# Turning B and X of a selective-scan mixer by VectorE and DRAM, and another order of work for three cross-attention tiles

## The reference, cut to what matters

```
xp = pad(x @ W_in[:1536].T)                       # C, B, X: 512 features each
conv_out = sum(xp[:, k:k+s, :] * conv_w[:, k] for k in range(4)) + conv_b
C_, B_, xin = split(conv_out)                     # 16 heads of 32
Y = ssd(xin, A, B_, C_)[0] / norm                 # scan of batch entry 0, rated for each of 2
x = ln(x + Y @ W_out.T)                           # x1
x = ln(x + softmax(q(x) k(ctx).T) v(ctx) @ o_w)   # x2
x = ln(x + slots_and_experts(x))
```

## Time and profile before

| | us |
|---|---|
| median of 3 runs | 1476.79 (1472.14 to 1482.0) |
| profiled execution, its own time | 1479.82 |
| its span, first to last instruction | 1478.0 |
| PE busy in the span | 1314.2 (89%) |
| DVE / ACT / POOL busy | 731.9 / 442.8 / 218.3 |
| mean granted TensorE clock | 0.935 |

### The profile page before, as it was taken

One profiled execution on the slowest core, in us unless ns is written; L12 is line 12 of the kernel. 1 busy time (PEld: TensorE's weight loads), 2 busy tenths in 40 slices (PEclk: granted clock), 3 DMA queues, 4 the chain that ended last, 5 costly groups with the idle time before them and its releaser, 6 DMA issues.

```text
span 1478.0 us, 25849 instructions
## 1 busy us (share of the span) xinstructions
PE 1314.2 (89%) x10117; PEld 773.0 (52%) x10117; DVE 731.9 (50%) x1450; ACT 442.8 (30%) x1159; POOL 218.3 (15%) x182
## 2 busy tenths in 40 slices
PE   7999999999998899999999989877667766779998
PEld 4777777777675676767777554211111111126553
DVE  1655666666786778788888742000000000004665
ACT  2335443444323434434444330000000000002544
POOL 1122210222021222122222210000000000002221
PEclk9999999999999999999999999887877778789999
DMA  9452443432567698788887678999999999994773
GB/s 344 162 158 54 118 116 87 127 105 83 156 178 226 208 296 232 230 245 235 252 243 238 185 272 349 416 416 427 426 424 427 426 428 424 426 418 143 220 230 119
DMA packets 133353, 379.50 MB, mean 257 GB/s; under 512 B 15675, under 2 KB 52667, under 8 KB 116104
## 3 DMA queue, kind: packets, MB, share of 16 engines
q1 hardware_dynamic: 128456, 363.51, 69.9%
q10 hardware_dynamic: 4800, 14.68, 3.1%
HBM read 310.77 MB, written 67.37 MB: 256 GB/s over the span
## 4 chain that ended last, share of the span: by engine, by line
PE 58%; DMA 25%; DVE 7%; issue 2%; ACT 2%; SPq 1%; POOL 1%; ACTq 0%; DVEq 0%; POOLq 0%
DMA all_ring<-in_e_Wg 21%; PE mxw_bank L184 10%; PE mix_scores L730 7%; PE mxw_bank L982 5%; PE mix_scores L1759 4%; PE mxw_bank L1019 4%; PE mxw_bank L2243 4%; PE mxw_bank L1048 4%; PE mxw_bank L1067 2%; PE mix_scores L1782 2%; PE mix_scores L2276 2%; PE mxw_bank L2276 2%; PE mxw_bank L1009 1%; DMA all_space<-scratch_probs 1%; PE mxw_bank L722 1%
## 5 line engine op out<-in xcount | busy, mean ns | idle before, releaser
L1759 PE MATMUL mix_scores<-all_ring,all_space 128*32 128x512 f32 x968 | 150.4, 722 | 76.3 <-DMA all_ring<-in_e_W 38.1
L1809 DVE TENSOR_TENSOR all_space<-all_space 128x512 f32<-128x512 f32 x16 | 11.1, 694 | 380.6 <-ACT all_space L1818 380.6
L184 PE MATMUL mxw_bank<-all_ring,all_space 128*128 128x256 f32 x768 | 179.8, 388 | 1.7 <-DMA all_space<-in_WinT 1.7
L184 PEld LDWEIGHTS mxw_bank<-all_ring,all_space 128*128 128x128 f32 x768 | 145.3, 193 | 33.3 <-issue 10.8
L1818 ACT ACTIVATE all_space<-mix_scores 128x512 f32<-128x512 f32 x32 | 19.1, 597 | 409.4 <-PE mix_scores L1768 409.4
L1759 PEld LDWEIGHTS mix_scores<-all_ring,all_space 128*32 128x32 f32 x968 | 31.2, 120 | 179.4 <-DMA all_ring<-in_e_Wg 68.1
L254 DVE SCALAR_TENSOR_TENSOR all_ring<-all_ring,all_space 128x256 f32<-128x256 f32 x192 | 84.5, 482 | 76.6 <-ACT all_ring L203 74.3
L1782 PE MATMUL mix_scores<-all_ring,all_space 128*32 128x512 f32 x480 | 112.7, 735 | 10.2 <-DVE all_space L1812 10.2
L1242 POOL TENSOR_TENSOR all_space<-all_space,all_more 128x1232 f32<-128x1232 f32 x32 | 72.6, 2268 | 326.9 <-DVE all_more L1157 326.9
L1019 PE MATMUL mxw_bank<-all_space 128*128 128x512 f32 x248 | 113.1, 599 | 2.1 <-ACT all_space L1135 2.1
L730 PE MATMUL mix_scores<-all_space,all_ring 128*128 128x512 f32 x240 | 105.4, 592 | 0.0
(11 more groups left out here) (313 smaller groups left out, 2061.2 us busy)
## 6 DMA issues: line engine op xcount, KB each, us to landing
all_ring<-in_e_W SPq DMA_DIRECT2D x55, 2048.0 KB, 24.7
all_ring<-in_e_Wg SPq DMA_DIRECT2D x28, 2048.0 KB, 26.2
scratch_probs<-all_more SPq DMA_DIRECT2D x32, 768.0 KB, 3.5
all_space<-scratch_probs SPq DMA_DIRECT2D x64, 256.0 KB
all_ring<-in_xT SPq DMA_DIRECT2D x8, 1024.0 KB, 9.2
all_ring<-scratch_rates SPq DMA_DIRECT2D x64, 128.0 KB, 4.3
all_z<-in_x SPq DMA_DIRECT2D x16, 512.0 KB, 5.2
scratch_x1T<-all_more SPq DMA_DIRECT2D x128, 64.0 KB, 1.8
```

Of the source, the lines that this page charges most:

```text
L184: last = nc.tensor.matmul(bank[:, i * BT:(i + 1) * BT], hold["win"][:, k, m * P:(m + 1) * P], hold["xT"][b % 2][:, k, :], start=(k == 0), ...
L1759: last = nc.tensor.matmul(bank[w][q * ROWS:(q + 1) * ROWS, :], hm[u][:, k, :], weights[k % 2][:, q * FQ:(q + 1) * FQ], start=(k == 0), sto ...
```

## The change

**Mixer.** For blocks 1 to 7 (chunks 2 to 15), PE no longer turns B and X. DVE turns all eight tiles of a block in 32 x 32 pieces with one instruction (`turn_block`, 128 x 2048), SP stores the result to a scratch tensor in four DMAs, waits for them, and loads two arrays of 128 x 1024, one for each chunk (`exchange`). ACT's `take_b` and DVE's `weigh_x` then read SBUF instead of PSUM. Chunks 0 and 1 stay with PE. So that B is there early, the pairs of a block come in the order X, B, C. DVE adds the taps of each pair one place later in the order of work, and ACT normalises behind its second pair; the exceptions for the last two chunks are gone. **Cross.** Steps 2 and 3 have an order of their own on PE and DVE, with scores one tile further ahead; ACT's queries move; the statistics of the last two chunks move; SP loads the probabilities of tile 2 ahead of storing turned x2 of tile 0. **Semaphores.** Some are merged; this changes no order.

```diff
-PAIRS = ((8, 9), (10, 11), (0, 1), (2, 3), (4, 5), (6, 7))
+PAIRS = ((8, 9), (10, 11), (4, 5), (6, 7), (0, 1), (2, 3))
...
+    def exchange(sp, b):
+        sp.wait_ge(s["tok_turned"], b)
+        to = io["tok"][b * BT:(b + 1) * BT, :].rearrange("(j f) n -> f j n", f=QUAD)
+        for a in range(HG):
+            sp.dma_start(to[:, :, a * BT:(a + 1) * BT], turned[a * HD:(a + 1) * HD, :, :, :].rearrange("f j m n -> f j (m n)")).then_inc(s["tok_stored"], 16)
+        sp.wait_ge(s["tok_stored"], 16 * HG * b)
+        for c in (2 * b, 2 * b + 1):
+            wait_later(sp, s["xs_done"], c - 1)
+            wait_later(sp, s["btok_done"], c - 1)
+            sp.dma_start(tok[c % 2][:].rearrange("p a m f -> p (a m f)"), io["tok"][c * P:(c + 1) * P, :]).then_inc(tok_in[c % 2], 16)
...
+    def turn_block(dve, b):
+        dve.wait_ge(s["convX"], NX * (b + 1))
+        dve.wait_ge(s["convCB"], NCB * b + 2)
+        wait_later(dve, s["tok_stored"], 16 * HG * (b - 1))
+        nc.vector.transpose(turned[:], hold["conv"][b % 2][:, GROUPS:, :].rearrange("p m (j t) -> p j m t", t=QUAD)).then_inc(s["tok_turned"], 1)
...
                 first["weigh_x"](dve, c)
                 first["mask_scores"](dve, c)
-                taps(q)
+                taps(q - 1)
+                if c % 2:
+                    first["turn_block"](dve, c // 2 + 1)
                 first["rate_outputs"](dve, c)
                 first["advance_state"](dve, c)
-                if c == END - 2:
-                    taps(q + 1)
+                taps(q)
                 if c:
                     first["norm"](dve, c - 1)
-                if c != END - 2:
-                    taps(q + 1)
+                taps(q + 1)
                 first["residual"](dve, c)
                 if c >= 2:
                     first["turn_rows"](dve, c - 2)
-                taps(q + 2)
...
+                if known(t, 3):
+                    turn_probs(dve, t + 1)
+                    add_tokens(dve, t - 3, 1 - u, 0)
+                    turn_x2(dve, t - 1, 1 - u)
+                    take_scores(dve, t + 2, False)
+                    first["norm"](dve, LATE_ROWS[t])
+                    slot_maxima(dve, t - 2, 0)
+                    denominators(dve, t + 2)
+                    residual(dve, t, u)
+                    slot_sums(dve, t - 2, u, 0)
+                    return
...
                 if t in LATE_ROWS:
                     first["normalise"](act, LATE_ROWS[t])
-                if ahead(t, 3) and t >= SEAM:
-                    take_queries(act, t + 3)
```

138 lines of the change are left out of this document (93 added, 45 removed).

## The result

The changed kernel takes **1458.18 us** in the median of four executions (1455.67 to 1460.76), the kernel before 1477.63 in the median of four (1472.14 to 1482.0): a ratio of 0.9861 with a 95% interval of 0.9832 to 0.9889, 19.5 us or 1.4%. The prediction said 1460.7, between 1452 and 1474. The profiled execution took 1460.47 with a span of 1458.7; that of before had 1478.0, so 19.3 us lie between the two traces.

A forecast was written before the change was run, and what follows sets the result against it. PE was taken to bound the kernel, busy 312.65 of 313.00 us in full chunks. Mixer -6.7 (-11.5 + 3.0 + 1.8) and cross tiles -9.4 sum to -16.1, from median 1476.8 to 1460.7 us; range 1452 to 1474.

The forecast's parts named there:

- signs of being wrong: Stated beforehand: an even chunk exceeding 22.5 us, or cross tiles 2 to 5 taking over 65 us.
- PE loses the turns: Mixer, chunks 2 to 13: each loses 0.96 us of turning matmuls on PE, -11.5 us in all.
- ACT in even chunks: Mixer, chunks 2 to 12: PE waits 0.5 us for ACT's slower copy of B from SBUF, +3.0 us in all.
- DVE in odd chunks: Mixer: DVE's block transpose, 2.4 us, stays hidden in all odd chunks but 13, so PE's output projection does not wait.
- The trip: Mixer: turned block through DRAM lands 21.6 us after the odd chunk's scores start (S); nothing paid in chunks 2 to 12.
- its edge: Latest landing of the block's load without delaying even chunks: 24.6 us after the odd chunk's scores start (S).
- The last block: Mixer's end: chunk 14's outputs start 24.9 us after chunk 13's scores, where it was 23.1: +1.8 us.
- Cross tiles: Tiles 2 to 5 take 60.5 us instead of 69.95: -9.4 us, 4.5 of it from PE's clock.
- The 1.99 for probabilities goes: Cross tile 2: loading probabilities ahead of storing turned x2 brings them 3 us earlier, removing PE's 1.99 us wait.
- (1, 2): Two rivals: only the cross tiles gain, 1467 us, chance 0.13; only the mixer gains, 1468 us, chance 0.15.
- (4): Rival: both halves better, no ACT wait, small end, no half clock: -11 and -12, 1454 us; chance 0.13.
- (3): Rival: the block's transfer through DRAM is late, costing up to +27 us in the mixer, 1488 us; chance 0.12.

The follow-up runs named there:

- order_only: Changed kernel with its new order of work, but PE turns B and X of every chunk and nothing goes through DRAM: median 1471.77 us, 0.9962 of before.
- turned_twice: Changed kernel with DVE transposing each block twice in a row, the second waiting for the first: 1466.07 us, timed once.
- pool_holds: Changed kernel where, in the step behind tile 2, GpSimd adds its bias only after DVE's slot maxima: 1460.51 us.
- probs_later: Changed kernel with SP loading tile 2's probabilities behind the stores of turned x2, as before: 1456.36 us in one execution, median 1458.46 when timed again.
- cross_only: Mixer of the kernel before with the changed kernel's cross steps: median 1471.30 us, ratio 0.9959 to the kernel before.

## Why the prediction was right, and where its terms were not

The total was 1458.2 for 1460.7, and both of its halves have the expected sign. That it came so close is in part luck: the mixer gave 3.3 us more than its -6.7, the cross tiles 1.5 less than their -9.4, and 1.4 of the 19.3 us between the traces lie ahead of the change. Of the signs of being wrong none came: no even chunk over 22.5 us, tiles 2 to 5 under 65.

- **PE loses the turns: -11.5, right.** S to S fell from a mean of 22.44 to 21.52 out of odd chunks; twelve times 0.92 is 11.0. `order_only` shows that nothing else in the mixer does it.
- **ACT in even chunks: +3.0, was +0.7.** This is the term that was most over-sized in the mixer. The copy from SBUF takes 0.65 us, not 0.76, so it ends 0.1 sooner, and even chunks last 0.12 longer than odd ones (PE's weight loads wait 1.5 us in all, partly hidden). The row it was priced from scales two halves by a factor per row (still 1.52 us for two after the change); a plain copy was nearer to the 0.59 from PSUM. The 0.3 us per chunk that I added for the hand-over did not exist apart from the wait.
- **DVE in odd chunks: no wait, right.** The transpose takes 2.31 us (2.4 said, from 1.78 for three quarters of its size), rating ends at S+9.9 (S+10.1), the residual at S+19.2 (S+19.5). At the upper end of 5.3 us it would have been paid for: `turned_twice` pays at 4.6.
- **The trip: inside its edge, right; its length over-sized.** Four issues took 3.1 us where 1.9 stood, but the stores landed in 4.2 us and not in 6.0. A median of another store of 512 KB rows had been taken; the lower end, 3.9, was the better row. The load landed near S+19.5, not S+21.6. The edge is S+25.0 (S+24.6 said).
- **The last block: +1.8, was +0.2 at the outputs and +0.36 at tile 0's scores.** B and X arrive with the residual, not 2 us behind it. Together the mixer gave 9.95 us, not 6.7.
- **Cross tiles: -9.4, was -7.4** in tiles 2 to 5, and -0.45 ahead of them. Tiles 3, 4 and 5 took 14.4, 13.0 and 13.6, against 13.6, 13.6 and 14.3: 41.0 for 41.5. The step that fell short is tile 2: 21.5 for 19.0. The wait before turning slot probabilities was 3.46 for 2.1. Two operations of DVE held by GpSimd add up to those 1.4 us; `pool_holds` takes one of them away and the wait falls by 0.7; for the rest only the addition speaks. Over the four tiles the waits came out as forecast and the clock did not: idle time of PE fell from 11.7 to 6.7 us, 5.1 for the 4.9 that the sum implies, while PE's busy time fell only from 58.2 to 55.9 us (52.0 at full clock), 2.3 for the 4.5 booked as clock. The largest piece of what is left is the token weighing of tile 2, at 3.78 us for 1.99: I had taken the half clock away with the waits, while waits of 1 to 3.5 us were still there.
- **"The 1.99 for probabilities goes": true and worth nothing by itself.** `probs_later` has that wait at 1.4 and the next one at 1.97 for 3.46 (1.05 in its second trace, where no operation of DVE was held). Two waits in a row on one engine were one wait for the slowest partner, DVE; taking the first away lengthens the second. Nor does the work behind tile 5 simply start earlier by what is gained, as the prediction had it: tiles 6 to 9 give 2.1 us back in these two traces, 2.3 in that of `cross_only`.
- **The rivals.** Neither half failed to come (1, 2): the mixer gave 9.95 us, the cross tiles 7.86. Of (4) the mixer's part nearly came (-11), the end of the half clock did not. The transfer's being late (3) is real, but from S+25.0 on; the Trainium skill's warning (VectorE: DVE Perf Modes, The three transpose paths) of a plain DMA copy that transposes by strides (19 times slower, there, than the DMA transpose) does not bear on it: the stores in runs of 1 KB landed in 4.2 us and the loads of 4 KB rows in 4.3. The fit of the Trainium skill (DMA: Bandwidth & Descriptors, Anatomy of one DMA), quoted in the prediction, gave as an estimate landings of 4.4 and 3.2 us and S+19: nearer to the measured S+19.5 than mine for the trip as a whole. Without proof are the -1.4 us ahead of chunk 1, which I count as scatter, and what sets PE's clock in tile 2.

## What to carry to other kernels

Matmuls that only turn data are worth their own time where PE is full, if another engine has the time at the right moment: count the deadline of the result, from the start of the step that wants it, and test it by making the trip longer. Far past the edge (6.65 us here) the time lost is more than the lateness, since PE's clock fell behind the long wait. And when one of several waits in a row on an engine is removed, ask what the next one waits for: if it is the same slow partner, nothing is gained. Follow the gain for some stages beyond the change as well: tile 6 took 3.8 us more here, waiting for a transfer. A difference of 2 us that hangs on PE's clock in a stretch needs more than one trace.
